# Attention and experts in one kernel: score units one at a position, and a few steps at other positions

## What is computed

```python
q, k, v = split_heads(x @ w_qkv.T)                     # 16 heads of 16
q, k = rope(rms_norm(q, q_norm_w), rms_norm(k, k_norm_w))
attn = softmax(causal(q @ k.T * scale))                # 512 x 512 per head
x = layernorm(x + (attn @ v) @ w_proj.T)
normed = x * rsqrt(mean(x * x) + 1e-8) * norm_weight
shared = relu(normed @ sw1 + sb1) @ sw2 + sb2
probs = sigmoid(normed @ router_w.T)                   # 8 logits a token
scores, idx = top_k(probs, 2)
routed = sum over the two experts of w * expert(normed)
out = layernorm(x + shared + routed)
```

## Time and profile before

| | |
|---|---|
| median of 3 runs | 939.65 us (939.44 to 940.9) |
| the profiled execution, its own time | 943.1 us |
| its span, first to last instruction | 941.4 us |
| TensorE busy | 882.9 us, 94% of the span |
| VectorE busy | 583.6 us, 62% |
| ScalarE busy | 613.7 us, 65% |
| GpSimd busy | 428.9 us, 46% |
| mean granted clock of TensorE | 0.985 |

### The profile page before, as it was taken

The page is one execution under the profiler, slowest core; times in us unless marked ns, Lnnn a source line. Parts: engine busy times, 40 slices in busy tenths (PEclk is TensorE's granted clock), DMA queues, the critical chain, the costliest instruction groups (busy, mean ns, idle before and its releaser), DMA issues.

```text
span 941.4 us, 26124 instructions
## 1 busy us (share of the span) xinstructions
PE 882.9 (94%) x9049; PEld 699.4 (74%) x9050; DVE 583.6 (62%) x1206; ACT 613.7 (65%) x1061; POOL 428.9 (46%) x602
## 2 busy tenths in 40 slices
PE   4778999999999979999999999999999999999997
PEld 1444556565556647888888999998999989898886
DVE  8653778988989747783554544444444432437976
ACT  4678988888988867343665555556655454666774
POOL 5342454778868627571234434344434344512311
PEclk8789999999999999999999999999999999999999
DMA  5120231415312256467883122121212111238751
GB/s 178 68 90 1 68 102 52 145 45 158 114 47 100 100 203 217 147 224 275 261 269 111 56 68 68 46 73 51 68 48 76 46 58 48 76 118 284 229 168 56
DMA packets 67601, 108.56 MB, mean 115 GB/s; under 512 B 7648, under 2 KB 45920, under 8 KB 67392
## 3 DMA queue, kind: packets, MB, share of 16 engines
q1 hardware_dynamic: 50144, 73.12, 23.9%
q10 hardware_dynamic: 10896, 16.40, 6.0%
q0 software_dynamic: 6480, 17.97, 5.3%
HBM read 64.48 MB, written 42.98 MB: 114 GB/s over the span
## 4 chain that ended last, share of the span: by engine, by line
PE 63%; POOL 11%; issue 8%; ACT 8%; DVE 6%; DMA 2%; another core or an unknown queue 1%; ACTq 0%; DVEq 0%; POOLq 0%; SPq 0%
PE yb L1916 24%; PE hb L1897 24%; ACT prob L884 4%; PE pv_bank L1681 3%; PE hb L1747 3%; POOL rsum L712 2%; PE tr L1767 1%; POOL xg_rows L753 1%; POOL rsum L709 1%; PE slot L1655 1%; POOL nat L727 1%; POOL vv L736 1%; DMA rs<-resid 1%; PE yb L1784 1%
## 5 line engine op out<-in xcount | busy, mean ns | idle before, releaser
L1056 ACT ACTIVATE hf<-hb,b 128x256 f32<-128x256 f32 (+1 forms) x392 | 154.6, 453 | 197.1 <-PE hb L1897 173.8
L1897 PE MATMUL hb<-xgT,wts 128*128 128x256 f16 (+1 forms) x1872 | 213.3, 263 | 1.9 <-ACT hf L1056 1.6
L1916 PE MATMUL yb<-wts,hh 128*128 x1704 | 210.6, 273 | 0.7 <-DVE hh L1485 0.6
L1485 DVE TENSOR_TENSOR hh<-hf,hh 128x1024 f16<-128x1024 f32 (+1 forms) x98 | 119.0, 1217 | 132.2 <-ACT hh L1061 107.3
L1897 PEld LDWEIGHTS hb<-xgT,wts 128*128 x1872 | 181.2, 98 | 21.3 <-issue 1.6
L819 POOL DMA_INDIRECT y_tok<-yb,dest x71 | 78.2, 1101 | 226.4 <-DVE yb L1497 209.6
L1916 PEld LDWEIGHTS yb<-wts,hh 128*128 128x128 f16 x1704 | 166.3, 98 | 19.7 <-DVE hh L1485 1.0
L884 ACT ACTIVATE prob<-slot 128x1024 f32<-128x1024 f32 x160 | 156.5, 1042 | 36.4 <-PE slot L1668 34.3
L1061 ACT ACTIVATE hh<-hf 128x1024 f16<-128x1024 f32 (+1 forms) x98 | 97.6, 996 | 3.1
L753 POOL DMA_INDIRECT xg_rows<-xnh,sl_i x64 | 74.9, 1170 | 15.4 <-issue 13.1
L1681 PE MATMUL pv_bank<-prob,vst 128*32 128x512 f32 (+3 forms) x1024 | 75.6, 436 | 0.5 <-ACT prob L884 0.5
(11 more groups left out here) (250 smaller groups left out, 1438.4 us busy)
## 6 DMA issues: line engine op xcount, KB each, us to landing
wts<-in_w_all SPq DMA_DIRECT2D x27, 512.0 KB
wts<-y_tok SPq DMA_DIRECT2D x32, 256.0 KB, 4.8
xg<-xg_rows ACTq DMA_DIRECT2D x30, 264.0 KB
xTf<-in_xT SPq DMA_DIRECT2D x8, 512.0 KB
stage<-in_w_all SPq DMA_DIRECT2D x8, 512.0 KB
w_split<-chunk_hl SPq DMA_DIRECT2D x8, 512.0 KB, 3.0
xin<-in_x SPq DMA_DIRECT2D x8, 512.0 KB
resid<-y SPq DMA_DIRECT2D x16, 256.0 KB
```

The source lines that it names most:

```text
L1056: act.activation(hf[:, c, 0:size], hb[c // 2][:, (c % 2) * TT:(c % 2) * TT + size], ACT.Relu, bias=bias, scale=1.0 / WS).then_inc(S("relu_ ...
L1485: dve.tensor_tensor(hh[:, par, 1, cs, 0:size], hf[:, cs, 0:size], hh[:, par, 0, cs, 0:size], ALU.subtract).then_inc(S("h_lo"), 1)
L1897: ins = pe.matmul(hb[hc // 2][:, (hc % 2) * TT:(hc % 2) * TT + size], weights(e, c, w, hc * P, P), xgT[:, par, x * DC + c, 0:size], start= ...
L1916: ins = pe.matmul(bank, hh[:, par, x, hc, P * j:P * j + P], weights(e, DC + hc * D // CH, w, hc * D % CH, D), start=(n == 0), stop=(n == H ...
```

## The change

What it does:

- At every position one unit: its scores, then its mask, and one exponential on ScalarE (`exps`).
- The q/k product of a tile at the start of a round (QK entry -20, from the third sequence on) is issued ahead of unit 0, no longer behind it.
- XN_ROWS goes from 38 to 40 for the first pair of tiles: behind the refinement and `normed` on VectorE.
- SPACED goes from (58, 60, 64, 66) to (58, 63, 65, 66): two scatters later.
- The low half of SPLIT_X on VectorE three positions behind the high one, not one.
- Chunks at 10, 30, ... 130 and 144, the low half two positions behind the high one.
- The router's weights are stored with both halves side by side, and one matmul of 16 columns takes the place of two of 8. VectorE adds the halves (`tensor_reduce` for `tensor_scalar`), and the factor 1/RS goes into the exponential's scale.

The diff, its core:

```diff
-XN_ROWS = (38, 43)
+XN_ROWS = (40, 43)
-SPACED = (58, 60, 64, 66)
+SPACED = (58, 63, 65, 66)
-CHUNK_AT = 6
-CHUNK_GAP = 18
+CHUNK_POS = (10, 30, 50, 70, 90, 110, 130, 144)
+CHUNK_LOW = 2
@@ ScalarE, step
                     for c, p in due(UNITS, g):
-                        if p % 2 == 0:
-                            exps(c, p)
-                            exps(c, p + 1)
+                        exps(c, p)
@@ VectorE, chosen
-                    then(dve.tensor_scalar(lg[:].rearrange("p t e -> p (t e)"), mc[:, 0:NT * NE], 1.0 / RS, None, ALU.mult),
+                    then(dve.tensor_reduce(lg[:], mc[:, 0:2 * NT * NE].rearrange("p (t y e) -> p t e y", y=2, e=NE),
+                                           AX.X, ALU.add),
@@ VectorE, step
-                    for c, _ in due(SPLIT_X, g - 1):
+                    for c, _ in due(SPLIT_X, g - 3):
-                    for k in chunk_due(g - 1):
+                    for k in chunk_due(g - CHUNK_LOW):
@@ TensorE, step
+                    for c, t in due(QK, g):
+                        if c >= 2 and position(QK, c, t) % NPOS == 0:
+                            pe.wait_ge(S("xT_lo"), c + NT)
+                            pe.wait_ge(S("ma_free"), NTH["qk", c, t])
+                            product(qk_bank(c, t), c, t, slice(0, 2 * D)).then_inc(S("qk_done"), 1)
                     for c, p in due(UNITS, g):
-                        if p % 2 == 0:
-                            for k in (p, p + 1):
-                                scores(c, k)
-                            for k in (p, p + 1):
-                                masked(k)
+                        scores(c, p)
+                        masked(p)
@@ TensorE, logits
-                        four = [(x, y, k) for k in range(DC) for x in range(2) for y in range(2)]
+                        both_halves = [(x, k) for k in range(DC) for x in range(2)]
                         for t in range(NT):
-                            for n, (x, y, k) in enumerate(four):
-                                last = pe.matmul(mc[:, t * NE:(t + 1) * NE], xnT[:, t // 2, x * DC + k, t % 2, :], wrout[:, y, k, :],
+                            for n, (x, k) in enumerate(both_halves):
+                                last = pe.matmul(mc[:, 2 * t * NE:2 * (t + 1) * NE], xnT[:, t // 2, x * DC + k, t % 2, :],
+                                                 wrout[:, k, :, :].rearrange("p y e -> p (y e)"),
```

More of the change, by code:

```diff
@@ L152 @@
 N_RAW = N_CHUNKS - len(CHUNKS)
-assert CHUNK_AT + (len(CHUNKS) - 1) * CHUNK_GAP <= EARLY_IN - 7 and len(CHUNKS) % 2 == 0
+assert len(CHUNK_POS) == len(CHUNKS) and CHUNK_POS[-1] + CHUNK_LOW <= EARLY_IN - 6 and len(CHUNKS) % 2 == 0
 def rows_due(g):
@@ L161, in chunk_due @@
 def chunk_due(g):
-    return [k for k in range(len(CHUNKS)) if CHUNK_AT + k * CHUNK_GAP == g]
+    return [k for k in range(len(CHUNKS)) if CHUNK_POS[k] == g]
 def early_order():
@@ L295, in program @@
         wproj = sb("wproj", [P, 2, DC, D], F16)
-        wrout = sb("wrout", [P, 2, DC, NE], F16)
+        wrout = sb("wrout", [P, DC, 2, NE], F16)
         ident_f = sb("ident_f", [P, P], F32)
@@ L861, in split_more @@
                     act.activation(wproj[:, 0, :, :], stage[:, :, w:w + D], ACT.Copy, scale=WS).then_inc(S("w_hi"), 1)
-                    act.activation(wrout[:, 0, :, :], stage[:, :, w + D:], ACT.Copy, scale=RS).then_inc(S("w_hi"), 1)
+                    act.activation(wrout[:, :, 0, :], stage[:, :, w + D:], ACT.Copy, scale=RS).then_inc(S("w_hi"), 1)
                 act.wait_ge(S("vst_one"), 1)
@@ L1026, in step @@
                         act.wait_ge(S("top_ready"), 4 * (c + 1))
-                        act.activation(ex[:], mx[:, :, 0:2], ACT.Exp, scale=-1.0).then_inc(S("ex_ready"), 1)
+                        act.activation(ex[:], mx[:, :, 0:2], ACT.Exp, scale=-1.0 / RS).then_inc(S("ex_ready"), 1)
                     for c, _ in due(SPLIT_X, g):
@@ L1154, in low_more @@
                     low(2, wproj, w, w + D, WS)
-                    low(3, wrout, w + D, w + D + NE, RS)
+                    low(3, wrout[:].rearrange("p k y e -> p y k e"), w + D, w + D + NE, RS)
                 dve.wait_ge(S("const_ready"), 2)
@@ L1802, in step @@
                     for c, t in due(QK, g):
+                        if c >= 2 and position(QK, c, t) % NPOS == 0:
+                            continue
                         if c >= 1:
@@ L1839, in step @@
                         pe.wait_ge(S("mc_free"), max(NTH["lg", c, 0], NTH["xn", c, 1] + 1))
-                        four = [(x, y, k) for k in range(DC) for x in range(2) for y in range(2)]
+                        both_halves = [(x, k) for k in range(DC) for x in range(2)]
                         for t in range(NT):
-                            for n, (x, y, k) in enumerate(four):
-                                last = pe.matmul(mc[:, t * NE:(t + 1) * NE], xnT[:, t // 2, x * DC + k, t % 2, :], wrout[:, y, k, :],
-                                                 start=(n == 0), stop=(n == len(four) - 1))
+                            for n, (x, k) in enumerate(both_halves):
+                                last = pe.matmul(mc[:, 2 * t * NE:2 * (t + 1) * NE], xnT[:, t // 2, x * DC + k, t % 2, :],
+                                                 wrout[:, k, :, :].rearrange("p y e -> p (y e)"),
+                                                 start=(n == 0), stop=(n == len(both_halves) - 1))
                         last.then_inc(S("lg_done"), 1)
```

## The result

| | before | after |
|---|---|---|
| median of 5 runs | 939.65 us | 930.38 us (928.71 to 932.86) |
| ratio, with its 95% interval | | 0.9887 (0.9872 to 0.9903) |
| profiled execution, own time | 943.1 us | 928.7 us |
| its span | 941.4 us | 927.0 us |
| busy: TensorE, VectorE | 882.9, 583.6 us | 885.2, 583.3 us |

The change makes the kernel faster by 1.1%, 9.3 us by the medians and 10.6 us by the ratio. One disturbed run of the kernel before is left out of the ratio. The two profiled executions differ by 14.4 us. The one of before was 3.4 us above its median, the one of after the fastest of its five.

What follows compares the result with a forecast made beforehand. TensorE, busy nearly always, was taken to bound the kernel by its instructions plus stops. Edges +15.2, logits -3.3 and stops -6.6, -10.3 and -6.0 gave -11.0 us, 928.6 us by the median; the range was 918 to 942.

Steps and rivals of the forecast that it cites:

- Term 1: Switches between 64-row scores and 128-row work on TensorE: 0.19 us for each of 80 pairs, +15.2 us.
- None of it hidden, since TensorE does nothing beside it: Step on TensorE's added mode edges: all of their 15.2 us, 1.9 a round, lengthens the time.
- the 166 ns of my estimate: Upper price for each of 160 more edges on TensorE, from a single matmul's constant part: 26.6 us in all.
- Term 2: Router logits on TensorE: 16 matmuls in place of 32 save 0.41 us a round, 3.3 us over 8 rounds.
- Term 3: TensorE's stops in the three stretches with units: 6.6, 10.3 and 6.0 us go.
- First: Stretch from 36.8 to 100 us: 6.6 us of stops go, mainly waits on exponentials and copies behind them.
- Second: Stretch from 100 to 311 us: of 16 us of stops 5.7 stay, 1.1 a round, and 10.3 go.
- Third: Stretch from 311 to 361.5 us, without q/k products: stops mostly on exponentials, about 9 us, of which 6 go.
- The edges are paid and the stops stay elsewhere: Rival: VectorE's and ScalarE's order only shifts lateness, a third to half of stops goes; 934.5 to 939.5 us, chance 0.20.
- The slower rival: The chunk on VectorE behind the logits makes TensorE's transposes wait 1.4 us each round; 946.5 us, chance 0.12.
- All stops go: Rival: 36 us of TensorE's stops less 3 go, first stretch's clock made whole; -21, 918.5 us, chance 0.10.
- The edges are not paid twice: Rival: mask and score units in turn cost less than 0.05 us an edge on TensorE; -19, 920 us, chance 0.03.

Runs made afterwards that it cites:

- d: The changed kernel with XN_ROWS, SPACED, the chunks and the low half of SPLIT_X at their old positions; 937.4 us, ratio 0.9958.
- c2: The changed kernel with neighbouring units issued as scores, scores, mask, mask where nothing stands between, except units 19 and 0; 928.29 us, ratio 0.9857.
- f: The changed kernel with the old logits, 32 matmuls of 8 columns in place of 16 of 16; 931.13 us, ratio 0.9893.
- b: The changed kernel with scores, masks and exponentials in pairs again, all other parts of the change kept; 930.38 us, ratio 0.9895.
- a: The kernel before with only the units changed: one unit of scores, mask and exponential at each position; 939.06 us, ratio 0.9975.
- i: c2 with the low half of each chunk made on VectorE for 8 of 1,024 columns only; 929.79 us, ratio 0.9851.
- k: c2 with the low half of SPLIT_X on GpSimd, one position earlier, and the second expert's scatters later; 941.35 us, ratio 0.9964.

## Why the prediction was right, and where its working was not

The forecast was 928.6 us, -11.0; measured were 930.38 and a ratio that makes -10.6. That stops caused by the order on VectorE, GpSimd and ScalarE go is what the trace and d show. That the sum came so near is partly luck: the edges (+15.2) and the stops (-22.9) were both taken as paid and won in full, both too large, and the two errors cancel. Taking 2.8 us for 106 of the 159 edges (c2) and 0.6 for the logits (f), the edges cost some 4 us and the stops are worth some 14, an estimate. And without the units, the part that costs the edges, the ratio is 0.9895 in place of 0.9887 (b).

**Term 1, the edges, +15.2.** The price was right: 0.11 and 0.10 an edge in the timeline, 1.09 for two lone units against 0.89 for a pair. The count was too: 353 changes of mode against 194. "None of it hidden, since TensorE does nothing beside it" is the step that failed. In middle rounds b, c2 and the changed kernel have different numbers of edges and take 40.0 us each. Taking 106 edges out brought 2.8 us instead of 10.1. I had read VectorE as near full and still let TensorE's work set the round. TensorE does nothing beside an edge, but it would otherwise wait at that time: c2 shows 1.4 us of stops in a middle round, 0.75 for `y` and 0.65 for ScalarE's copies, the changed kernel 0.45, all for `y`. With the other engines' order as before (a), part of the edges was paid: the middle rounds are 0.8 longer. The Trainium skill ("TensorEngine Tiling (Array Packing)", Key Properties) says that a change of mode drains the engine. The trace agrees, with about 0.1 us a change, not the 166 ns of my estimate.

**Term 2, the logits, -3.3.** The saving in place is 0.87 - 0.48 = 0.39, as forecast. It came to 0.6 us in f, less than the runs tell from nothing, for the same reason: TensorE gets to the `mb` transposes earlier and waits there for `y`.

**Term 3, the stops, -22.9.** Shown were 12.4 + 11.6 + 7.0 = 31.0 us, and 12.9 are left: 18.1 shown are gone. By stretch:

- *First:* forecast -6.6 for stops, +2.7 for edges. Measured -5.5 shown, and 7.1 us shorter in all. The difference is the clock, 0.92 to 0.97. TensorE's busy time should have risen by the 2.7 (28 units) and fell by 1.5, about 4 us to explain. The two PEclk values make 10.1 us at 1.2 GHz before and 3.4 after; what ran in these 6.7 us takes up to 3.4 less at 2.4 GHz, so the clock explains most. The kernels that issue all scores in pairs have the lower share, the others a higher one (see b); that it is shorter stops that raise it was not tried by itself. The forecast named that only in a rival. The exponentials' waits fell from 5.7 to 3.2, the 2.6 on `vst` to 2.0 only, the 2.0 on `sq` to 0.6, and the 1.9 on the stack became 0.9 at the product ahead.
- *Second:* 11.6 to 1.7 shown. I had let 5.7 of 16 stay. The three new waits were placed rightly: `xnh` 0.2 (0 to 0.2), `mb` on `y` 0.6 (0.1 to 0.7, taken 0.4), `nat` none where I kept 0.3. The middle rounds are 40.0 and 40.2, forecast about 40.3, but it is not TensorE's work that sets them.
- *Third:* forecast 6 of 9 gone, net about -4; the stretch is 1.7 us shorter and 4.3 of stops are shown, 3.8 of them on exponentials (2.7 by scores, 1.1 by attention values). "Mostly those on exponentials" was right, that lone units end them was not. The likely reason, not tried, is that without q/k products too little stands between two units for ScalarE to catch up.

**The parts do not add.** The units alone bring 2.3 us, the rest alone 11.0 by its median (9.9 by its ratio), both together 10.6. The moves on VectorE and GpSimd are worth 6.7 us within the change, the q/k product ahead 0.8. In the profiles the units bring 3.1 us up to LG0, lose 0.9 in the five rounds and 1.1 behind them; by the medians nothing is left.

**The rivals.** "The edges are paid and the stops stay elsewhere" is what a shows; what remained there are waits for VectorE's `an` and GpSimd's `nat`, which d has too and the moves take out. The slower rival, the chunk as a wait each round, has its mechanism in the trace: VectorE comes late to the logits, and TensorE waits for `y`. But it waits 0.6 us, not 1.4, below the 0.7 from which I let it decide. "All stops go" is nearly true of the second stretch and of no other. "The edges are not paid twice" is false of the price of an edge; most of the edges cost no time all the same.

## What to carry to other kernels

Before work on a nearly full engine is priced, find out whose order sets the stage: take a little work from each engine in turn and see which one shortens a round, and look at the busy times of the others too, since they can move with it, as GpSimd's did here. What is added to or taken from the others is then paid only beyond their slack. With queues in order, what another engine waits for belongs ahead of what nobody waits for, here the refinement ahead of the experts' rows and chunks behind the logits; those moves brought most of the gain. And where two engines hand slots to each other, both orders must be changed together: one side alone cost 31 us.

## What the runs showed of the hardware

- A switch between 64-row and 128-row matmuls costs about 0.1 us of TensorE at 2.4 GHz, in either direction, for pairs and lone units alike. Matmuls of 8 and of 16 columns take the same time, about 0.025 us.
- The same VectorE instruction varies: the low half of a chunk took 1.46 us in the earlier trace rows and 1.81 here, `rot` 1.20 at 224.44 and 0.69 at other places of the round. GpSimd is busy beside both. What runs on one of the two engines changes the times on the other: with the chunk's low half cut to 8 columns (i), 16 `rsum` instructions of GpSimd take 14.5 us in place of 16.3 in c2, and beside a GpSimd subtraction of 2.15 us (k) an instruction of VectorE takes 2.58 us in place of 0.22.
- 128 x 1,024 fp32 less fp16 takes 1.22 us on VectorE and 2.15 us on GpSimd.
- Near the end of the units TensorE stopped up to 1.14 us between independent matmuls with no release shown, in some kernels and not in others.
